# Two transformer layers on one core: the gate's limit of the second experts is taken by ScalarE, as a Relu of 7 minus bias minus gate

## The reference

```
gate_up = einsum('nd,ejd->nej', x, gate_up_proj) + gate_up_proj_bias
gate, up = split(gate_up, 2)
gate = minimum(gate, 7.0)
up = clip(up, -7.0, 7.0)
act = (up + 1.0) * gate * sigmoid(1.702 * gate)
out = einsum('nei,edi->ned', act, down_proj) + down_proj_bias
y = einsum('ned,ne->nd', out, combine)
```

## Time and profile before

| | |
|---|---|
| median of 3 runs | 2818.09 us (2817.61 to 2819.32) |
| the profiled execution | 2820.42 us, span 2818.7 us |
| busy: PE, DVE | 2497.2 us (89%), 2185.9 us (78%) |
| busy: ACT, POOL | 1441.5 us (51%), 719.1 us (26%) |
| L1146, 256 times | 191.0 us |
| L757, 256 times | 160.6 us, idle before it 468.8 us |
| wait of PE's weight load of L1343 for L1146 | 87.2 us |

### The profile page before, as it was taken

How to read it: one execution, slowest core, us unless ns; L and a number is a source line. 1 busy time by engine, 2 the same in 40 slices (tenths; PEclk the granted TensorE clock), 3 DMA queues, 4 the chain that set the end, 5 groups by cost and what they waited for, 6 DMA issues and landing times.

```text
span 2818.7 us, 67301 instructions
## 1 busy us (share of the span) xinstructions
PE 2497.2 (89%) x26720; PEld 1807.0 (64%) x26720; DVE 2185.9 (78%) x3781; ACT 1441.5 (51%) x2616; POOL 719.1 (26%) x593
## 2 busy tenths in 40 slices
PE   4988989889898898988989889899898998989989
PEld 2766657675566665666667666576665766667656
DVE  4958878589786897777977779767797687985878
ACT  2746237563375534665246642566435573365723
POOL 1220342204322042220522215122151121520225
PEclk8999999999999999999999999999999999999999
DMA  6110211102111021110201112011120101201012
GB/s 224 39 37 4 87 49 39 38 2 98 38 39 38 2 102 35 39 38 25 82 31 42 35 39 75 24 46 31 47 71 26 44 27 54 68 27 47 19 63 65
DMA packets 93370, 136.25 MB, mean 48 GB/s; under 512 B 10111, under 2 KB 55240, under 8 KB 92552
## 3 DMA queue, kind: packets, MB, share of 16 engines
q1 hardware_dynamic: 84872, 115.16, 12.5%
q0 software_dynamic: 8192, 16.79, 2.0%
HBM read 101.31 MB, written 30.61 MB: 47 GB/s over the span
## 4 chain that ended last, share of the span: by engine, by line
PE 62%; DVE 19%; issue 11%; ACT 6%; POOL 2%; DVEq 0%; ACTq 0%; POOLq 0%
PE ps L1475 10%; PE ps L1343 8%; PE ps L1511 7%; PE ps L1417 6%; PE ps L1496 5%; DVE neg_max L1028 5%; PE ps L1548 4%; PE ps L1350 4%; PE ps L1439 3%; DVE probsT L1036 3%; ACT probs L701 2%; PE ps L1364 2%; PE ps L1317 2%; DVE ffn L1163 1%; PE ps L1428 1%
## 5 line engine op out<-in xcount | busy, mean ns | idle before, releaser
L1028 DVE TENSOR_REDUCE neg_max<-ps 128x1 f32<-128x1024 f32 x512 | 623.2, 1217 | 48.6 <-PE ps L1475 38.9
L701 ACT ACTIVATE probs<-ps,neg_max 128x1024 f32<-128x1024 f32 x512 | 571.6, 1117 | 156.3 <-DVE neg_max L1028 154.5
L1475 PE MATMUL ps<-keys,q_parts 64*128 64x512 f32 x3072 | 520.2, 445 | 82.8 <-ACT probs L701 57.0
L1343 PE MATMUL ps<-q_parts,w_split 128*128 128x512 f32 x1536 | 458.5, 435 | 42.6 <-DVE ffn L1146 24.0
L1496 PEld LDWEIGHTS ps<-ident,probs 64*128 64x128 f32 x8192 | 347.2, 143 | 96.4 <-ACT probs L701 17.3
L1343 PEld LDWEIGHTS ps<-q_parts,w_split 128*128 128x128 f32 x1536 | 284.7, 192 | 191.9 <-DVE ffn L1146 87.2
L1475 PEld LDWEIGHTS ps<-keys,q_parts 64*128 64x128 f32 x3072 | 264.1, 196 | 220.4 <-ACT probs L701 109.2
L600 POOL TENSOR_TENSOR probs<-ffn,q_parts 128x512 f32<-128x512 f32 x208 | 294.7, 1418 | 429.3 <-DVE ffn L1163 291.9
L757 ACT ACTIVATE ffn<-ffn 128x512 f32<-128x512 f32 x256 | 160.6, 630 | 468.8 <-DVE ffn L1146 468.4
L1036 DVE COPY probsT<-ps 128x512 f32<-128x512 f32 x512 | 348.6, 681 | 23.6 <-PE ps L1496 23.6
L1496 PE MATMUL ps<-ident,probs 64*128 64x64 f32 x8192 | 350.1, 227 | 16.4 <-ACT probsT L683 16.2
(11 more groups left out here) (213 smaller groups left out, 3297.0 us busy)
## 6 DMA issues: line engine op xcount, KB each, us to landing
w_split<-w_parts SPq DMA_DIRECT2D x132, 256.0 KB, 2.6
q_parts<-gate_rows SPq DMA_DIRECT2D x64, 512.0 KB, 4.0
y_rows<-probs SPq DMA_DIRECT2D x40, 256.0 KB, 2.2
x_in<-in_x SPq DMA_DIRECT2D x9, 512.0 KB, 4.3
w_parts<-q_parts SPq DMA_DIRECT2D x2, 2048.0 KB, 13.7
out<-x_mid SPq DMA_DIRECT2D x8, 512.0 KB, 3.2
ffn<-in_gate_up SPq DMA_DIRECT2D x1, 2048.0 KB, 8.9
probsT<-in_gate_up SPq DMA_DIRECT2D x1, 2048.0 KB, 13.1
```

The source lines that it names most:

```text
L701: nc.scalar.activation(probs[:, t % 3, :], banks(2 * (t % 2)), ACT.Exp, bias=neg_max[:, t % 4:t % 4 + 1], accum_out=row_sum[:, g % 2, t % ...
L1028: nc.vector.tensor_reduce(neg_max[:, t % 4:t % 4 + 1], banks(2 * (t % 2)), X, ALU.max, negate=True).then_inc(max_ready.sem, 1)
L1343: mm = nc.tensor.matmul(ps[:, bank, :], w_split[:, f % CHUNK_SLOTS, h, k * P:(k + 1) * P], tokens[:, half], start=(part == 0), stop=(part ...
L1475: mm = nc.tensor.matmul(ps[:, 2 * (t % 2) + c, :], q_parts[rows, j, q, n * P:(n + 1) * P], keys[rows, k, :], start=(part == 0), stop=(part ...
```

## The change

ACT now reads the gate bank itself: it computes Relu(room - gate), with room = 7 - bias prepared once per run (`room_of_gate`), which is 7 minus the limited gate. The Silu then takes scale -1.702 and bias 1.702 * 7, so that its argument is again 1.702 times the limited gate. The bias, which was a constant in the instruction, is now a column in memory (`silu_bias`). DVE keeps the up's limit alone. The copy of the gate weights stands behind the Relu of unit 0. The signal `gate_lim`, for which PE waits, now comes from ACT.

```
+            act.wait_ge(limits_ready.sem, 2)
...
-                copy_gatesT(b)
                 for u in range(UNITS):
+                    act.wait_ge(gu_ready.sem, gu_ready.at(b, u + 1))
+                    nc.scalar.activation(ffn_g[:, u % 3, :], ps[:, u % 2, :], ACT.Relu, scale=-1.0,
+                                         bias=room_of_gate[:, u // HALVES:u // HALVES + 1]).then_inc(gate_lim.sem, 1)
+                    if u == 0:
+                        copy_gatesT(b)
...
-                    nc.scalar.activation(ffn_s[:, u % 3, :], ffn_g[:, u % 3, :], ACT.Silu, scale=ALPHA
+                    nc.scalar.activation(ffn_s[:, u % 3, :], ffn_g[:, u % 3, :], ACT.Silu, scale=-ALPHA,
+                                         bias=silu_bias[:, 0:1]
                                          ).then_inc(silu_done.sem, 1)
...
+            nc.vector.memset(silu_bias[:, :], ALPHA * LIMIT).then_inc(limits_ready.sem, 1)
             dve.wait_ge(weights_in.sem, ALL_WEIGHTS)
+            nc.vector.tensor_scalar(room_of_gate[:, :], b_gate[:, :], -1.0, LIMIT, ALU.mult, ALU.add
+                                    ).then_inc(limits_ready.sem, 1)
...
                     dve.wait_ge(gu_ready.sem, gu_ready.at(b, u + 1))
-                    if u >= 3:
-                        dve.wait_ge(silu_done.sem, silu_done.at(b, u - 2))
-                    nc.vector.tensor_scalar(ffn_g[:, u % 3, :], ps[:, u % 2, :], b_gate[:, f:f + 1], LIMIT,
-                                            ALU.add, ALU.min).then_inc(gate_lim.sem, 1)
```

More of the change, by code:

```diff
@@ L289, in two_layer_kernel @@
         b_gate = sb("b_gate", [P, E * FH])
+        room_of_gate = sb("room_of_gate", [P, E * FH])
+        silu_bias = sb("silu_bias", [P, 1])
         b_up = sb("b_up", [P, E * FH])
@@ L406, in two_layer_kernel @@
         gate_lim = signal("gate_lim", UNITS)
+        limits_ready = signal("limits_ready")
         up_lim = signal("up_lim", UNITS)
```

## The result

The changed kernel takes 2789.1 us (median of 6 runs, 2787.9 to 2801.7), the kernel before beside it 2815.8 (2813.2 to 2819.3). The ratio is 0.9912, with a 95% interval of 0.9893 to 0.9931: 25 us faster, between 19 and 30 (the two medians lie 26.6 us apart). A second set of runs gave 0.9905 (0.9889 to 0.9922). The forecast was 31 us. The profiled execution has 2787.4 us of span, 31.3 less than the one before; two single profiles differ by that much, the medians by a little less.

A forecast was written before the change was run, and what follows sets the result against it. VectorE was taken to set the pace from unit 5 to 20 of layer 2's expert stage. Gains of 0.9, 2.9, 1.6 and 0.3 less 1.9 give 3.8 us a sequence, about 31 us in all: 2787 us, range 2768 to 2804.

The forecast's parts named there:

- The bound: Layer 2's expert stage: VectorE sets the pace from unit 5 to 20; at most about 8 us a stage to win.
- Prices: A removed limit frees 0.66 us of VectorE; ScalarE's Relu costs 0.68 and Silu 0.73 us, hidden in PE's 2.26 us unit.
- Start of the stage: Up to PE's first sums: 0.9 us gained, from qkv rounds 0.3 us earlier plus the 0.57 us wait.
- Unit 5 to the second sums: Six gate limits leave VectorE's chain, 4.0 us; two collisions with POOL take 0.66 and 0.42, leaving 2.9 us gained.
- Second sums to T: Up to T, the end of L1223: three gate limits go, 2.0 us, 0.45 lost to POOL; 1.6 us gained.
- The detour: After L1223 ends, PE waits for Relus behind ScalarE's Tanh, Exp, loads and copies; 1.9 us lost by unit 20.
- End: Last products and POOL multiplies of the stage: 0.3 us gained, between 0 and 0.66.
- Sum: 3.5 + 0.3 = 3.8 us a sequence, about 31 us over eight, giving 2787 us; chance 0.5.
- Rival 1: Collisions with POOL do not come or move elsewhere: about 5.7 us a sequence, 2772 us; chance 0.23.
- rival 2: ScalarE's longer chain after L1223, or two more collisions, leaves 1.5 to 2 us a sequence: 2804 us; chance 0.14.
- rivals 3 and 4: 3: no change, waits move to ScalarE, 2818 us, chance 0.06. 4: two table loads a unit, 2980 us, chance 0.05.

The follow-up runs named there:

- relu_twice: The changed kernel with each Relu done twice on ScalarE, the first time into scratch that nobody reads; 2796.7 us, ratio 0.992.
- no_limit_gates_later: The changed kernel without the gate's upper limit (Silu straight from the bank), gate-weight copy behind the Silu of unit 0; 2793.0 us, ratio 0.9909.
- ahead_sigmoid_first: relu_ahead, with VectorE also turning the Tanh into sigmoids before product 2 instead of behind it; 2765.0 us, ratio 0.981.
- no_gate_limit: The changed kernel without the gate's upper limit (Silu straight from the bank), gate-weight copy ahead of everything in unit 0; 2824.7 us, ratio 1.0019.
- relu_ahead: The changed kernel with the Relus of units 16, 17 and 18 moved earlier in ScalarE's queue; 2772.3 us, ratio 0.9834.

## Why the prediction was right

**The bound.** Right: VectorE set the pace from unit 5 to the second sums. With it relieved the groups of PE moved up: units 8 to 11 follow their predecessors after 2.25, 2.54, 2.48 and 2.85 us, where it was 3.54, 3.22, 3.13 and 3.22. With POOL's work small PE ran there at its own 2.25 us a unit.

**Prices.** Right within 0.01 us for the two activations, and the two kernels with small POOL work bear out the 0.66 us of a limit (4.06 us for six, below). That the pair is hidden in the ordinary unit was shown by relu_twice and by no_limit_gates_later.

**Start of the stage, 0.9 forecast, 0.30 measured.** The one term that was mis-sized. PE's chain came 0.3 us earlier, as forecast: `gate_up(2)` starts 4.3 us after `gate_up(0)` instead of 4.6, since the up's limit of unit 0 no longer stands behind a gate's limit; the qkv rounds behind it took the same (4.0 us to `gate_up(3)` in both). But the 0.57 us wait for the sigmoids stayed (0.53 us), and the forecast had given PE all of it. It named product 2 as beginning while POOL works and put no price on that: the product lasts 1.32 us instead of 0.68, and this 0.64 us eats the limit that was taken from in front of it. Product 1 had met POOL in the kernel before too (1.14 us, now 1.29). The sigmoids stand behind both products. ahead_sigmoid_first gains by it.

**Unit 5 to the second sums, 2.9 forecast, 3.07 measured.** Right, with its two hold-ups: 1.90 us for product 9 (0.67 lost, 0.66 forecast) and 0.97 for product 7 (0.29 lost, 0.42 forecast). The gate limits alone would have been worth 4.0 us. The two kernels with small POOL work differ by 25.87 - 21.81 = 4.06 us here.

**Second sums to T, 1.6 forecast, 1.88 measured.** Right; product 14 lasted 0.98 us instead of 0.68, and L1190 won 0.3 us (1.75 instead of 2.02) that I had left out.

**The detour, -1.9 forecast, -1.77 at unit 20 and -0.33 behind it.** Right, and shown by undoing it. (The terms for the Relu of 17 add up to T + 6.4, not the 6.3 that the forecast went on with; it ended at T + 6.1.) The 0.33 us were missed: unit 20's group started after a gap and lasted 1.63 us, and now it stands right behind `down(15)` and lasts 1.96. Groups of about 1.63 us also stand behind short turns without a gap (1396.18 in the kernel before), so a wait is not all that makes the difference, and no run here isolates it.

**End, 0.3 forecast, 0.37 measured.** Right.

**Sum.** 3.8 us a sequence forecast, 3.5 by the steps of the fourth sequence and 3.85 on the mean of eight. The last is so near by luck, since 0.3 us of it is the slow first sequence of the kernel before. The steps give 28 us and the runs 25 to 27, against 31; the start alone was over-rated by 0.6 us a sequence, 5 us in all. That the time came within 2 us of the forecast 2787 is luck too: the kernel before, run beside it, took 2815.8 us and not the 2818.1 from which the forecast was reckoned. Rival 1 (no collisions) is what the kernels with small POOL work show; rival 2 (a dearer detour) did not come, and rivals 3 and 4 neither. What the forecast said of VectorE's busy time was wrong: 170 to 190 us less expected, 100.8 measured, since far more products than the three on the path were lengthened by POOL (product 23 alone from 0.68 to 2.68 us), and since each limit had held only 0.66 us of busy time. More than half of the added time lies behind T, where no step of PE from unit 22 on grew.

## What to carry to other kernels

Work taken from the bound engine is worth its time there only as far as the next thing behind it doesn't wait for the same neighbour: count, for each place where an instruction moves up, whether what it moves into is free. On the engine that gets the work the amount may be free while its place in the queue is not; look at which release now stands behind which wait, table load and copy. A release that other engines wait for belongs ahead of them. And look at what follows a longer wait: in no_gate_limit the 3.09 us for which PE stood still cost another 1.6 us by the granted clock behind them.

## What the runs showed of the hardware

- A product of two operands in the on-chip memory waits until POOL's operation is over: in the fourth sequence of both kernels each product that was lengthened ended 0.55 us behind the end of a POOL operation. On the path that cost 0.3 to 1.2 us (0.68 to 1.90 for product 9), at most 2.0 (product 23). The reverse holds too: POOL's multiply lasts 1.28 us alone and 2.18 where VectorE's L1182 or its one-input sigmoids (L1192) began 0.16 us before it. Beside the reductions (L1186), which began as early, it kept 1.28 us.
- Two activations that read the same bank one after the other start 0.57 us apart, though each lasts 0.68.
- Between equal sequences of one run PE's time scattered by up to 5 us, by the granted clock. In the sixth sequence of relu_ahead the first sums ran at 1.2 GHz for about 6 us. Before it PE had been busy 3.45 us of 4 and had waited for the sigmoids (columns as in the earlier trace rows):

```profile
1994.00:1998.00 4.00, 3.45 (x9) 1.01 (x7) 4.00 (x4) 3.54 (x4) 2.75 (x3) 0.97 0.99 370
1998.00:2002.00 4.00, 3.57 (x8) 2.86 (x9) 2.05 (x3) 0.00 (x0) 2.76 (x2) 0.50 0.02 7
```

  First to second sums took 26.7 us there, 23.7 in most others. This scatter sits mostly in the start of the stage, less often behind the first sums, and between the stages. Differences of 5 us between medians here therefore prove little without the steps of the stage beside them.
